# A wavelet convolution: two images side by side on the 128 partitions in the second pass

## What is computed

```python
yl, yh = _dwt2(x, 4)
yl_out = einsum('bixy,ioxy->boxy', yl, w_yl)                   # 42 x 42 coefficients
yh_out = yh[:-1] + [einsum('bicxy,iocxy->bocxy', yh[-1], w_yh)]
out = _idwt2(yl_out, yh_out)
# what the kernel computes: out = x + S @ delta @ S.T, delta = mixed - own, 84 x 84 for each image
```

## Time and profile before

| | |
|---|---|
| median of three runs | 2003.56 us (2002.23 to 2013.93) |
| the profiled execution | 2001.11 us, its span 1999.5 us |
| PE, DVE, ACT, POOL busy | 93%, 41%, 24%, 7% of the span |
| moved by DMA | 827.12 MB, 414 GB/s over the span |
| pass 2 | from about 750 us to the end |

### The profile page before, as it was taken

The page is one execution under the profiler, slowest core; times in us unless marked ns, Lnnn a source line. Parts: engine busy times, 40 slices in busy tenths (PEclk is TensorE's granted clock), DMA queues, the critical chain, the costliest instruction groups (busy, mean ns, idle before and its releaser), DMA issues.

```text
span 1999.5 us, 44393 instructions
## 1 busy us (share of the span) xinstructions
PE 1859.7 (93%) x17652; PEld 931.5 (47%) x17652; DVE 810.1 (41%) x930; ACT 480.8 (24%) x1047; POOL 132.2 (7%) x249
## 2 busy tenths in 40 slices
PE   6999999999999899999999999999999999999996
PEld 3656666666666554444343343343343343333332
DVE  2222222222222445555444444444444444444443
ACT  1223232332332551131121121121121121122110
POOL 0000000000000000011111111111111111111110
PEclk9999999999999999999999999999999999999999
DMA  9999999999999898999999999999999999999997
GB/s 395 399 369 405 421 422 422 421 422 422 422 422 422 335 400 361 373 427 427 427 427 427 427 427 427 427 427 427 427 427 427 427 427 427 428 424 417 424 426 335
DMA packets 114216, 827.12 MB, mean 414 GB/s; under 512 B 12688, under 2 KB 12688, under 8 KB 16912
## 3 DMA queue, kind: packets, MB, share of 16 engines
q1 hardware_dynamic: 79344, 573.01, 68.9%
q0 software_dynamic: 34848, 253.77, 30.3%
HBM read 558.29 MB, written 268.44 MB: 413 GB/s over the span
## 4 chain that ended last, share of the span: by engine, by line
DMA 58%; PE 33%; issue 4%; DVE 2%; SPq 1%; ACT 0%; DVEq 0%; POOLq 0%; ACTq 0%
DMA out<-x_sb 32%; DMA x_sb<-x 26%; PE ps L376 11%; PE ps L522 8%; PE ps L389 6%; PE ps L512 2%; DVE x_sb L757 2%; PE ps L473 2%; PE ps L468 1%; PE ps L400 1%; SPq L300 1%; PE ps L408 1%; PE ps L423 1%; ACT mix_sb L572 0%; PE ps L482 0%
## 5 line engine op out<-in xcount | busy, mean ns | idle before, releaser
L522 PE MATMUL ps<-spread,const 128*128 128x512 f32 x2048 | 940.0, 602 | 73.5 <-DVE x_sb L757 73.5
L757 DVE TENSOR_TENSOR x_sb<-ps,x_sb 128x1024 f32<-128x1024 f32 x500 | 592.7, 1220 | 630.0 <-DMA x_sb<-x 543.0
L522 PEld LDWEIGHTS ps<-spread,const 128*128 128x128 f32 x2048 | 373.4, 190 | 637.7 <-issue 407.5
L669 ACT COPY spread<-ps 84x512 f32<-84x512 f32 x256 | 149.0, 582 | 921.8 <-PE ps L512 920.3
L376 PE MATMUL ps<-x_sb,const 32*32 32x512 f32 x8192 | 290.2, 601 | 37.4 <-DMA x_sb<-x 30.8
L389 PEld LDWEIGHTS ps<-const,work 128*128 128x128 f32 x2048 | 246.5, 193 | 54.6 <-ACT work L557 40.2
L512 PE MATMUL ps<-const,pick 128*84 128x512 f32 x512 | 261.3, 592 | 1.0 <-issue 1.0
L389 PE MATMUL ps<-const,work 128*128 128x84 f32 x2048 | 255.4, 277 | 2.0 <-ACT work L557 2.0
L275 POOL DMA_DIRECT2D x_sb<-x x242 | 128.6, 532 | 1841.5 <-DMA out<-x_sb 1841.5
L557 ACT COPY work<-ps 128x512 f32<-128x512 f32 x256 | 131.4, 599 | 411.1 <-PE ps L376 411.1
L376 PEld LDWEIGHTS ps<-x_sb,const 32*32 32x32 f32 x8192 | 138.5, 103 | 138.8 <-issue 99.3
(11 more groups left out here) (26 smaller groups left out, 270.8 us busy)
## 6 DMA issues: line engine op xcount, KB each, us to landing
x_sb<-x SPq DMA_DIRECT2D x256, 1024.0 KB, 10.0
out<-x_sb SPq DMA_DIRECT2D x250, 1024.0 KB, 24.6
x_sb<-x POOLq DMA_DIRECT2D x242, 1024.0 KB, 11.7
work<-w_full SPq DMA_DIRECT2D x30, 896.0 KB, 7.2
work<-x SPq DMA_DIRECT2D x6, 1024.0 KB, 5.9
out<-work SPq DMA_DIRECT2D x6, 1024.0 KB, 9.8
work<-w_left SPq DMA_DIRECT2D x1, 896.0 KB, 15.0
const<-consts SPq DMA_DIRECT2D x1, 888.0 KB, 4.7
```

The costliest lines, as they stand in the source:

```text
L522: last = nc.tensor.matmul(ps[:, 2 + k], const[:, SH + P * k:SH + P * k + P], spread[:, p], start=True, stop=True)
L669: nc.scalar.copy(spread[0:ROWS, p], ps[0:ROWS, p]).then_inc(s_copied[p], 1)
L757: nc.vector.tensor_tensor(part, ps[:, 2 + 2 * half:4 + 2 * half], part, ALU.add).then_inc(added[half], 1)
```

## The change

From turn 2 on two images share a slot pair. `pair_sb` views slots 2s and 2s+1 as one buffer in which a partition holds 16 KB, eight neighbouring rows of one image; the first image of the pair is on partitions 0 to 63, the second on 64 to 127. Each image is still one load of 1 MB and one store of 1 MB, now on 64 partitions.

- POOL issues two loads for a slot pair, each after the store of the same half.
- SP waits until DVE has added both images, then issues two stores.
- PE's `pair_stage(c)` makes the four rows of a slot for both images: for each bank two matmuls with 64 columns of the synthesis matrix (every second column), one for each image, in place of one with 128. So both images' `spread` are needed before the first step of a pair; `spread` gets four buffers, and PE and ACT prepare it one image further ahead.
- DVE's two adds for each slot stay as they are; at the first slot of a pair it waits for both loads.
- Turns 0 and 1 stay as they were, and the loops for turns 2 and 3 of the first batch are written out.

```diff
+    x_pairs = x.rearrange("b (n h) (p r) w -> (b n) (h p) r w", h=2, r=2 * ROW_RUN)
+    out_pairs = out.rearrange("b (n h) (p r) w -> (b n) (h p) r w", h=2, r=2 * ROW_RUN)
...
+        pair_sb = x_sb[:].rearrange("p (s h) r w -> p s (h r) w", h=2)
...
+            return spread_sb[:, c % 4] if c % 4 < 2 else more_spread[:, c % 4 - 2]
...
+            def refill_half(s, h, t, first):
+
+                c = 2 * s + h
+                pool.wait_ge(x_stored[c], 16 * (t - (c < EARLY)))
+                part = slice(P // 2 * h, P // 2 * h + P // 2)
+                pool.dma_start(pair_sb[part, s], x_pairs[first + s, part]).then_inc(x_reloaded[c], 16)
+
             for c in range(SLOTS):
-                if c < EARLY:
-                    refill(c, 2, IMAGES - 3 * SLOTS)
-                else:
+                if c >= EARLY:
                     refill(c, 1, IMAGES - 2 * SLOTS)
-            for c in range(EARLY, SLOTS):
-                refill(c, 2, IMAGES - 3 * SLOTS)
+                elif c % 2:
+                    pool.wait_ge(x_stored[c], 16)
+                    for h in range(2):
+                        refill_half(c // 2, h, 2, (IMAGES - 3 * SLOTS) // 2)
+            for c in range(EARLY, SLOTS, 2):
+                pool.wait_ge(x_stored[c + 1], 32)
+                for h in range(2):
+                    refill_half(c // 2, h, 2, (IMAGES - 3 * SLOTS) // 2)
             with pool.Fori(3, TURNS) as t:
-                first = t * -SLOTS + (IMAGES - SLOTS)
-                for c in range(SLOTS):
-                    refill(c, t, first)
+                first = t * (-SLOTS // 2) + (IMAGES - SLOTS) // 2
+                for s in range(SLOTS // 2):
+                    for h in range(2):
+                        refill_half(s, h, t, first)
...
             with sp.Fori(2, TURNS) as t:
-                first = t * -SLOTS + (IMAGES - SLOTS)
-                for c in range(SLOTS):
-                    store(c, t, first)
+                first = t * (-SLOTS // 2) + (IMAGES - SLOTS) // 2
+                for s in range(SLOTS // 2):
+                    sp.wait_ge(added[1], SLOTS * t + 2 * s + 3)
+                    for h in range(2):
+                        part = slice(P // 2 * h, P // 2 * h + P // 2)
+                        sp.dma_start(out_pairs[first + s, part], pair_sb[part, s]).then_inc(x_stored[2 * s + h], 16)
...
+            def pair_stage(c, t):
+
+                u, n = c % 2, SLOTS * t + c
+                for h in range(2):
+                    pe.wait_ge(s_copied[h], SLOTS // 2 * t + c // 2 + 2)
+                for half in range(2):
+                    pe.wait_ge(added[half], n + 1)
+                    for k in (2 * half, 2 * half + 1):
+                        for h in range(2):
+                            last = nc.tensor.matmul(ps[64 * h:64 * h + 64, 2 + k], const[:, SH + P * k + u:SH + P * k + P:2],
+                                                    spread(c - u + h), start=True, stop=True)
+                    last.then_inc(o_done[half], 1)
...
+            def copy_spread_pair(c, t):
+                p, n = c % 2, SLOTS // 2 * t + c // 2
+                act.wait_ge(s_done[p], n + 1)
+                act.wait_ge(o_done[1], SLOTS * t + 2 * (c // 2) - 1)
+                nc.scalar.copy(spread(c)[0:ROWS], ps[0:ROWS, p]).then_inc(s_copied[p], 1)
...
             with dve.Fori(2, TURNS) as t:
                 for c in range(SLOTS):
-                    dve.wait_ge(x_reloaded[c], 16 * (t - (c < EARLY)))
+                    if c % 2 == 0:
+                        for h in range(2):
+                            dve.wait_ge(x_reloaded[c + h], 16 * (t - (c < EARLY)))
                     add(c, t, x_sb[:, c])
```

More of the change, by code:

```diff
@@ L160, in wavelet_mix_kernel @@
         x_sb = sb("x_sb", [P, SLOTS, ROW_RUN, SIZE])
+        pair_sb = x_sb[:].rearrange("p (s h) r w -> p s (h r) w", h=2)
         mix_sb = sb("mix_sb", [P, STEPS, 4, ROWS, BATCH])
         pick = sb("pick", [P, 2, ROWS])
-        spread = sb("spread", [P, 2, SIZE])
+        spread_sb = sb("spread_sb", [P, 2, SIZE])
         first_stage = const[:, 0:Q * ROWS]
@@ L196, in wavelet_mix_kernel @@
         delta = work[:, 2 * IMAGE:at].rearrange("p (a r) -> p a r", r=ROWS)
-        assert at + STEPS * Q * ROWS <= AT_EARLY
+        AT_SPREAD = AT_EARLY - 2 * SIZE
+        assert at + STEPS * Q * ROWS <= AT_SPREAD and AT_DIAG + 2 * 4 * U * QB <= AT_SPREAD
+        more_spread = work[:, AT_SPREAD:AT_EARLY].rearrange("p (a w) -> p a w", a=2)
         stage = work[:, at:at + STEPS * Q * ROWS].rearrange("p (v r) -> p v r", v=STEPS)
@@ L207, in wavelet_mix_kernel, with spread @@
         LAST_BANKS = (4, 5, 6, 7, 3, 2)
+        def spread(c):
+            return spread_sb[:, c % 4] if c % 4 < 2 else more_spread[:, c % 4 - 2]
         def diag_of(k):
@@ L268, in _ @@
             nc.gpsimd.memset(pick[:], 0.0).then_inc(cleared, 1)
-            nc.gpsimd.memset(spread[:], 0.0).then_inc(cleared, 1)
+            nc.gpsimd.memset(spread_sb[:], 0.0).then_inc(cleared, 1)
+            nc.gpsimd.memset(more_spread, 0.0).then_inc(cleared, 1)
             def refill(c, t, first):
@@ L521, in out_stage @@
                     for k in (2 * half, 2 * half + 1):
-                        last = nc.tensor.matmul(ps[:, 2 + k], const[:, SH + P * k:SH + P * k + P], spread[:, p],
+                        last = nc.tensor.matmul(ps[:, 2 + k], const[:, SH + P * k:SH + P * k + P], spread(c),
                                                 start=True, stop=True)
+                    last.then_inc(o_done[half], 1)
[9 more added lines that the diff above has]
+                                                    spread(c - u + h), start=True, stop=True)
                     last.then_inc(o_done[half], 1)
@@ L527, in turn2 @@
                 for c in range(SLOTS):
-                    if c < SLOTS - 1:
-                        spread_stage(c + 1, t)
+                    if c < SLOTS - 2:
+                        spread_stage(c + 2, t)
                     elif not last:
-                        spread_stage(0, t + 1)
-                    out_stage(c, t)
+                        spread_stage(c + 2 - SLOTS, t + 1)
+                    pair_stage(c, t)
                     if batch is not None and 1 <= c <= 3:
@@ L535, in turn2 @@
                         coefs_stage(2 * (c - 1) + 1, batch)
-            pe.wait_ge(cleared, 3)
+            pe.wait_ge(cleared, 4)
             spread_stage(0, 0)
-            with pe.Fori(0, BATCH - 1) as k:
+            for c in range(2 * SLOTS):
+                spread_stage((c + 1) % SLOTS, (c + 1) // SLOTS)
+                out_stage(c % SLOTS, c // SLOTS)
+            spread_stage(1, 2)
+            turn2(2)
+            turn2(3, batch=1)
+            with pe.Fori(1, BATCH - 1) as k:
                 with pe.Fori(0, TURNS_BATCH - 1) as r:
@@ L550, in _ @@
                 act.sem_inc(s_copied[a], 1)
-            act.wait_ge(cleared, 3)
+            act.wait_ge(cleared, 4)
             def copy_h(a, t, m):
@@ L668, in copy_spread @@
                 act.wait_ge(o_done[1], SLOTS * t + c)
-                nc.scalar.copy(spread[0:ROWS, p], ps[0:ROWS, p]).then_inc(s_copied[p], 1)
+                nc.scalar.copy(spread(c)[0:ROWS], ps[0:ROWS, p]).then_inc(s_copied[p], 1)
[3 more added lines that the diff above has]
+                act.wait_ge(o_done[1], SLOTS * t + 2 * (c // 2) - 1)
+                nc.scalar.copy(spread(c)[0:ROWS], ps[0:ROWS, p]).then_inc(s_copied[p], 1)
             def turn2(t, last=False, batch=None):
@@ L675, in turn2 @@
                         copy_delta(2 * (c - 2) + 1, batch, None)
+                    if c < SLOTS - 3:
+                        pick_image(c + 3, t)
+                    elif not last:
+                        if batch is not None and c == SLOTS - 3:
+                            act.wait_ge(d_copied, STEPS * (batch + 1) + IDLE + 1)
+                        pick_image(c + 3 - SLOTS, t + 1)
                     if c < SLOTS - 2:
-                        pick_image(c + 2, t)
+                        copy_spread_pair(c + 2, t)
                     elif not last:
[L679 to L685, removed]
+                        copy_spread_pair(c + 2 - SLOTS, t + 1)
                     if batch is not None and c <= 2:
@@ L694, in _ @@
             copy_spread(0, 0)
-            with act.Fori(0, BATCH - 1) as k:
+            for c in range(2 * SLOTS):
+                pick_image((c + 2) % SLOTS, (c + 2) // SLOTS)
+                copy_spread((c + 1) % SLOTS, (c + 1) // SLOTS)
+            pick_image(2, 2)
+            copy_spread_pair(1, 2)
+            turn2(2)
+            turn2(3, batch=1)
+            with act.Fori(1, BATCH - 1) as k:
                 with act.Fori(0, TURNS_BATCH - 1) as r:
```

## The result

The change makes the kernel slower by 9%: the ratio to the kernel before is 1.0901, interval 1.0859 to 1.0943, a median of 2207.2 us in four runs. The time of 2002 us and the range of 1984 to 2100 us were both wrong.

The account below looks back on a forecast made before the run. The prediction took the DMA engines to set pass 2's pace (4.91 us an image at 427 GB/s). Terms -7 + 0 + 0 + 2 + 3 = -2 us on the 2003.56 us median gave about 2002 us, range 1984 to 2100.

Parts of the forecast that it names:

- part 2: Pass 2 transfers on 64 partitions each: no cost taken for the steady part; bounds nothing to +1178 us.
- rival 1: Pass 2 transfers by halves hinder each other: 2025 to 2100 us, or 2590; chances 0.16 small loss, 0.17 over 5%.
- the small loss: Milder case of rival 1 in pass 2: 2 to 8% of pace lost, 2025 to 2100 us; chance 0.16.
- Part 1: Loads and stores of 240 images: half as many data packets, 16 KB runs, saving 7 us; bounds nothing to 14.
- Part 3: PE's sixteen 64-column matmuls per image: 3.4 us plus 0.1 to 0.2, PE's pace 4.5 us, cost nothing.
- Rival 2: PE becomes the bound in pass 2: +94 us, 2098 us, or +670 us without overlap; chance 0.09.
- Part 4: Coarser slots: no new wait in steady pass 2, +2 us at the start, +3 at the end.
- Rival 3: DMA engines even out, the late one's 6 us go, edges give 14 us: -20 us, 1983; chance 0.08.

Follow-up runs that it names:

- e1_whole: The changed kernel, but each pair is one load and one store of 2 MB over all 128 partitions in 16 KB runs; 2008.17 us, ratio 1.0021 to the kernel before.
- e8_whole_again: The kernel of e1_whole unchanged, run once more for a second profile; 2005.48 us in one run.
- e2_slots: The changed kernel's pair layout and pair stage, but one 1 MB transfer per slot, 128 partitions, 8 KB runs; 2010.61 us, ratio 1.0009 to the kernel before.

## Why the prediction was wrong

- **The step that failed is part 2**, "I take nothing for the steady part". Its working was right up to the last line: each direction needs 213.5 GB/s, and the question was whether a half of the partitions can take that. It takes 205, or 212 when loads go to the halves in turn, so the point from which rival 1 decides was passed before any question of phases. This shortage is the smaller part: two ways at 205 to 212 would carry 410 to 424 GB/s together, by estimate 8 to 49 us more for 240 images than at 427. The rest of the 181 us comes when loads and stores by halves run side by side: each way then carries 184 as the mean of the stretch (368 together), and even on opposite halves 387 together. That they hinder each other is measured. By which wait they do is open; a fixed limit for each way isn't the whole of it, since stores by halves in turn reach 428 GB/s when they are alone. I called it balance where it was a margin of nothing, on one half of a resource that no row had shown at its limit.
- **Rival 1 was the outcome, with its price mis-sized.** Arbitrary phases with nothing to even them out gave 1.5 times and 2590 us; the small loss gave 2 to 8%. Measured was 1.15 times the time of the transfers (425 to 368 GB/s), 9% of the whole. Its marks came as named: share at 1.0, GB/s falling, packets of 0.80 and 0.70 us against twice 307 ns. The chances gave 0.17 to a loss of over 5%, and the range left that out. A range drawn from this rival's own arithmetic would have gone beyond 2100.
- **Part 1 was right in kind.** I took 3.7 ns for a packet's edge. 427 against 431 GB/s in the two kernels' best windows is 4.911 against 4.866 us for an image's 2.097 MB, 45 ns for eight data packets and one completion fewer on each engine, 5 ns each. But this is a gain of 11 us only if held, and e1_whole's ratio of 1.0021 shows that it isn't. So the 7 us of the sum were not there, even without the halves. The 16 KB packets of the earlier trace rows were rightly given no weight. The bound of 1.9% on what packets can bring is worked out from the ceiling in the Trainium skill (DMA: Bandwidth & Descriptors, Where 436 GB/s comes from); that section doesn't state it.
- **Part 3 was right, a little short.** 3.66 us for the pair stage (3.4 plus up to 0.2 was taken) and 4.61 us for PE's pace (4.5), still under 4.87. Rival 2 didn't happen.
- **Part 4 was right in the steady part**: e1_whole, whose slots are as coarse, has a ratio of 1.0021. The start was taken at 2 us and is 7 in e8_whole_again, of which 2 are in e2_slots too. At the end the changed kernel's last load lands at 2195.9 us, as this row of its timeline shows, and 20.0 us remain until the span's end, where it was 13.9: 6 us, the top of the 0 to 6 that part 4 gave, taken at 3.

```profile
2195.88 2.36 DVE L815 TENSOR_TENSOR x_sb<-ps,x_sb 128x1024 f32<-128x1024 f32 x2 [5.70 <-DMA x_sb<-x]
```

- **Rival 3** rested on one late engine and on nothing that the change does; no run showed it.

## What to carry to other kernels

Transfers on partitions 0 to 63 ran at half the rate (205 GB/s against 426), and so did those on 0 to 31; if the kernel is bound by DMA, lay a smaller transfer over all 128 partitions or over every second one. When two needs are "just balanced" against a capacity that no row of the trace has tested, treat it as a loss until measured: a short kernel of transfers alone showed this one and its size. Read such a kernel by windows inside its stretches too: the mean of 379 GB/s for stores by halves hid a full rate of 428. In the profile of the changed kernel a DMA share of 1.0 beside falling GB/s went with packets of 0.80 and 0.70 us in place of 0.61, which issuing earlier can't cure; a share under 1, as the 0.91 at the start of pass 2 in e8_whole_again, is idle time of the DMA engines.

## What the runs showed of the hardware that I hadn't expected

- Stores by halves in turn reach the full rate by themselves (428 GB/s after their first 30 us), loads don't (212 of 419).
- Yet in the kernel loads by halves (1.0886) cost as much as both (1.0901), and stores by halves 1.0496.
- Packet length matters on a contended half: together by halves in turn, 4, 8 and 16 KB runs gave 401, 375 and 368 GB/s as means of their stretches, the reverse of what their edges alone would give. In these stretches only the runs of 16 KB lost pace on the way (410, then 363).
- In the pass 2 that is slowed by DMA, PE waits longer for DVE (up to 3.5 us at a time from 1000 to 1950 us, before up to 0.5 us) and its granted clock falls at times to the lower level: 0.94 as a mean from 1400 to 1600 us, 0.56 in the stretch of 7 us that followed a wait of 2.99 us, where before it was 1.00 throughout pass 2 until near its end.
